# Splitting a dependency name in the layer norm and moving the first half's output store in a transformer layer on eight cores

## What is computed

```python
# x: (4, 4096, 1024)
x = x + 0.5 * ffn(layernorm(x), W1, b1, W2, b2)
x = x + attn(layernorm(x), Wq, Wk, Wv, Wo)
x = x + 0.5 * ffn(layernorm(x), W1, b1, W2, b2)

# ffn: weights are rounded to -1, 0, 1 first (clip(round(W / (mean|W| + 1e-5))))
h = relu(x @ quant(W1).T + b1)          # 1024 -> 4096
out = h @ quant(W2).T + b2              # 4096 -> 1024
# attn: 16 heads of 64; a query sees the keys of its own block of 64
#       and the 16 global keys at the start, causally
```

## Time and profile before

| what | value |
|---|---|
| times of the two runs shown | 2217.58 and 2296.53 us, median 2257.06 us |
| device time of the profiled execution | 2216.75 us |
| its span, core 0 (slowest) | 2215.2 us |
| spans of the eight cores | 2201.8 to 2215.2 us |
| TensorE busy | 1531.6 us, 69% of the span |
| mean granted TensorE clock, core 0 | 0.828 of full speed |

### The profile page before, as it was taken

The page is one execution under the profiler, slowest core; times in us unless marked ns, Lnnn a source line. Parts: engine busy times, 40 slices in busy tenths (PEclk is TensorE's granted clock), DMA queues, the critical chain, the costliest instruction groups (busy, mean ns, idle before and its releaser), DMA issues.

```text
span 2215.2 us, 22369 instructions; the slowest of 8 cores (2201.8 to 2215.2 us)
## 1 busy us (share of the span) xinstructions
PE 1531.6 (69%) x8576; PEld 726.5 (33%) x8676; DVE 547.6 (25%) x746; ACT 423.2 (19%) x601; POOL 84.8 (4%) x68
## 2 busy tenths in 40 slices
PE   1003124861984797898956987989569879895698
PEld 0001001430444343343533433435334334354343
DVE  4663553001034300202043002020430020204300
ACT  1001001212203220311222303112223031122230
POOL 0000000000003000000030000000300000003000
PEclk7556556985895898898968998999689989996799
DMA  6877886783112145342220444422204544222044
GB/s 195 289 266 252 257 251 199 237 266 143 53 62 77 38 148 167 103 152 76 76 77 19 152 152 134 152 76 77 77 17 147 154 139 147 82 76 77 6 148 151
DMA packets 218496, 297.31 MB, mean 134 GB/s; under 512 B 6164, under 2 KB 194582, under 8 KB 215064
## 3 DMA queue, kind: packets, MB, share of 16 engines
q1 hardware_dynamic: 188056, 253.93, 36.5%
q10 hardware_dynamic: 30336, 41.95, 5.7%
HBM read 262.31 MB, written 33.55 MB: 134 GB/s over the span
## 4 chain that ended last, share of the span: by engine, by line
PE 58%; DMA 20%; DVE 10%; ACT 5%; issue 4%; POOL 2%; SPq 0%; ACTq 0%; DVEq 0%; POOLq 0%
PE PSB L391 17%; PE PSB L346 17%; PE PSB L463 10%; PE PSB L482 5%; DMA w2q_s<-xsq 3%; PE PSB L749 3%; DMA vaug<-w2t 3%; DMA w1b<-w1q_s 2%; POOL psb L599 2%; DMA w1q_s<-xsq 1%; PE SA L222 1%; DMA xres<-xfm 1%; DMA h<-w1t 1%; DMA vaug<-wvt 1%; DMA vaug<-wkt 1%
## 5 line engine op out<-in xcount | busy, mean ns | idle before, releaser
L346 PE MATMUL PSB<-xhat,w1b 128*128 128x512 bf16 x2003 | 477.5, 397 | 147.8 <-DMA w1b<-w1q_s 115.8
L391 PE MATMUL PSB<-h,w2b 128*128 128x512 bf16 x2001 | 453.2, 381 | 19.0 <-DMA w2b<-w2q_s 14.3
L346 PEld LDWEIGHTS PSB<-xhat,w1b 128*128 128x128 bf16 x2048 | 203.4, 101 | 402.6 <-issue 187.0
L391 PEld LDWEIGHTS PSB<-h,w2b 128*128 128x128 bf16 x2048 | 196.0, 98 | 259.7 <-issue 35.3
L351 ACT ACTIVATE h<-PSB,b1s 128x512 bf16<-128x512 f32 x256 | 176.0, 687 | 530.7 <-PE PSB L346 291.3
L402 DVE SCALAR_TENSOR_TENSOR xres<-PSB,xres 128x512 f32<-128x512 f32 x64 | 44.3, 692 | 877.7 <-PE PSB L396 770.9
L463 PE MATMUL PSB<-xhat,pjb 128*64 128x512 bf16 x1024 | 230.3, 389 | 11.9 <-DVE xhat L268 11.9
L463 PEld LDWEIGHTS PSB<-xhat,pjb 128*64 128x64 bf16 x1024 | 114.8, 112 | 126.6 <-issue 23.5
L222 PE MATMUL SA<-xsq,onesmean 128*1 128x512 bf16 x96 | 36.1, 544 | 138.3 <-ACT xsq L214 138.3
L489 DVE CAST vaug<-PSB 64x512 bf16<-64x512 f32 x64 | 43.7, 683 | 293.2 <-PE PSB L482 290.2
L482 PE MATMUL PSB<-pjb,xhat 128*64 128x512 bf16 x512 | 112.8, 382 | 4.1 <-DVE vaug L489 4.1
(11 more groups left out here) (122 smaller groups left out, 966.8 us busy)
## 6 DMA issues: line engine op xcount, KB each, us to landing
w1b<-w1q_s SPq DMA_DIRECT2D x64, 1024.0 KB, 6.5
w2b<-w2q_s SPq DMA_DIRECT2D x64, 1024.0 KB, 6.3
h<-w1t SPq DMA_DIRECT2D x16, 2048.0 KB, 9.0
vaug<-w2t SPq DMA_DIRECT2D x32, 1024.0 KB, 6.5
pjb<-wk_s SPq DMA_DIRECT2D x10, 1024.0 KB, 6.0
xres<-xfm SPq DMA_DIRECT2D x8, 1024.0 KB, 7.3
pjb<-wq_s SPq DMA_DIRECT2D x8, 1024.0 KB, 10.5
pjb<-wv_s SPq DMA_DIRECT2D x8, 1024.0 KB, 6.0
```

The lines of the kernel that those rows point to most:

```text
L346: lambda e, lhs=lhs, c=c, pview=pview: e.matmul(pview, lhs, xhat[:, c * T:(c + 1) * T], start=(c == 0), stop=(c == NCH - 1)),
L391: lambda e, buf=buf, c2=c2, pview=pview: e.matmul(pview, buf[:, c2 * 128:(c2 + 1) * 128], h[:, c2 * T:(c2 + 1) * T], start=(c2 == 0), stop ...
```

## The change

It has two parts.

First, the two ScalarE copies of `ln` also write names of their own, `xb_lo` and `xb_hi`. The matmuls of L222 read `xb_lo` for the first four chunks and `xb_hi` for the last four, in place of `xb`. The squaring L217 reads both, so it waits for the same as before. No instruction moves in any engine's list; a wait does.

Second, the output store is recorded inside `ffn2`, in the call whose result is final (`store_t=t`, the second `ffn2` of each tile): the first half behind the addition for `k` = 3, the second behind that for `k` = 7. The transfer `w2dma(5)` is recorded at the end of iteration 3, so it stands behind the first half's store.

```diff
         def ln(xr, xrname, glob):
             em.op("scalar", ... activation(xsq[:, 0:2048], xr[:, 0:2048], AF.Copy),
-                  reads=["xr_lo"], writes=["xb"])
+                  reads=["xr_lo"], writes=["xb", "xb_lo"])
             em.op("scalar", ... activation(xsq[:, 2048:4096], xr[:, 2048:4096], AF.Copy),
-                  reads=["xr_hi"], writes=["xb"])
+                  reads=["xr_hi"], writes=["xb", "xb_hi"])
             em.op("vector", ... xsq * xsq
-                  reads=["xb"], writes=["sq"])
+                  reads=["xb_lo", "xb_hi"], writes=["sq"])
             for c in range(NCH):
                 em.op("tensor", ... L222
-                      reads=["xb", "onesmean"], writes=bk(0))
+                      reads=["xb_lo" if c < 4 else "xb_hi", "onesmean"], writes=bk(0))
...
-        def ffn2(xr, xrname, glob):
+        def ffn2(xr, xrname, glob, store_t=None):
...
+                if store_t is not None and (k == 3 or k == 7):
+                    hf = 0 if k == 3 else 1
+                    dst = bass.AP(yout.tensor, (hf * 4) * 128 * TOK + store_t * T,
+                                  [[TOK, 128], [128 * TOK, 4], [1, T]])
+                    dma(lambda e, dst=dst, xr=xr, hf=hf: e.dma_start(dst, ...),
+                        reads=[f"xr_{half}"], writes=[f"yout{store_t}{hf}"],
+                        sem=f"ys{hf}")
...
-                    ffn(xr, xrname, False)
-            for hf in range(2):
-                dma(... store of half hf ..., sem=f"ys{hf}")
+                    ffn(xr, xrname, False, store_t=t)
```

More of the change, by code:

```diff
@@ L405, in ffn2 @@
                       reads=bank + [f"xr_{half}"], writes=[f"xr_{half}"])
+                if store_t is not None and (k == 3 or k == 7):
+                    hf = 0 if k == 3 else 1
+                    dst = bass.AP(yout.tensor, (hf * 4) * 128 * TOK + store_t * T,
+                                  [[TOK, 128], [128 * TOK, 4], [1, T]])
+                    dma(lambda e, dst=dst, xr=xr, hf=hf: e.dma_start(
+                        dst, xr[:, hf * 4 * T:(hf * 4 + 4) * T].rearrange(
+                            "p (c k) -> p c k", c=4)),
+                        reads=[f"xr_{half}"], writes=[f"yout{store_t}{hf}"],
+                        sem=f"ys{hf}")
                 if glob:
@@ L427, in ffn2, with ffn @@
                     w2dma(k + 2)
-        def ffn(xr, xrname, glob):
+        def ffn(xr, xrname, glob, store_t=None):
             ffn1(xr, xrname, glob)
-            ffn2(xr, xrname, glob)
+            ffn2(xr, xrname, glob, store_t=store_t)
         def proj(glob):
@@ L986, in build_nc @@
                     ln(xr, xrname, False)
-                    ffn(xr, xrname, False)
-            for hf in range(2):
[L989 to L995, removed]
+                    ffn(xr, xrname, False, store_t=t)
+                else:
+                    for hf in range(2):
+                        dst = bass.AP(yout.tensor, (hf * 4) * 128 * TOK + t * T,
+                                      [[TOK, 128], [128 * TOK, 4], [1, T]])
+                        dma(lambda e, dst=dst, xr=xr, hf=hf: e.dma_start(
+                            dst, xr[:, hf * 4 * T:(hf * 4 + 4) * T].rearrange(
+                                "p (c k) -> p c k", c=4)),
+                            reads=[f"xr_{'lo' if hf == 0 else 'hi'}"],
+                            writes=[f"yout{t}{hf}"], sem=f"ys{hf}")
         em.final_wait(["ys0", "ys1"])
```

## The result

The profiled execution of the changed kernel took 2238.58 us, its longest span 2237.0 us; before it was 2216.75. Over repeated runs of both kernels the ratio after to before is 1.0101, with a 95% interval from 1.0081 to 1.0122. The change makes the kernel slower by 1.0%. That lies within the 2% of the forecast, but the forecast was no change, and this is clearly not nothing. Predicted were 2236 us, a ratio of 1.0087 to the profiled execution. Some executions are several per cent slower whatever the kernel, by its time also the one of 2296.53 us shown before, and the ratios leave them out.

What follows compares the result with a forecast made beforehand. TensorE held 58% of the chain of waits, DMA 20%, VectorE 10%. To 2216.75 us it added 8.0 for the norms, 8.8 for waits at chunk 5 and 2.1 for clock falls: 2236 us, range 2207 to 2270.

Steps and rivals of the forecast that it cites:

- no change: Whole kernel: 2236 us, 0.9% above the profiled execution, was taken as within the 2% a measurement can tell; chance 0.92.
- the sum: Whole kernel: 2216.75 + 8.0 for the norms + 8.8 for the waits + 2.1 for the clock = 2235.7 us.
- L228's clock level: Layer norm: half clock in L228 makes its 8 matmuls 3.57 us instead of 1.89, a norm 6.1 instead of 4.43.
- the norm term: Twelve layer norms, L217's to L237's start: ten at half clock in L228 give 70.0 us, +8.0; bounds -8.8 and +11.4.
- The 62.0: Twelve norms before the change, in us: 44.0 without idle time plus 11.1 idle ahead of L232 and 6.9 ahead of L237.
- the load norms: First norms of tiles 1 to 3, behind a tile load: four matmuls run early at L211's end, too thin to help.
- The store's position: Second `ffn2`, chunk 5: weights behind 1 MB of store on the same queue land 8.0 us after issue; alone, 5.2.
- the piling-up rival: Chunks 5 and 6 of the second `ffn2`: store and three weight transfers pile up, both wait, +48 us, 2265 us; chance 0.06.
- The move brought nothing elsewhere: Tile end, next tile's loads and chunk 7's weights: moving the store gains nothing; a shorter tile boundary would refute it.
- The size of the wait: Chunk 5 of the second `ffn2`: a stall of 2.2 us in each of four tiles, 8.8 us, bounds 0 and 13.6.
- the clock's chance: Behind the wait at chunk 5: one time in three the clock falls, about 1.6 us each, 2.1 us in four tiles.
- The rule on gaps: Layer norms: long idle gaps between matmul bursts lower the clock; read alone, it favours the change, norms summing to 53.2 us.

Runs made afterwards that it cites:

- the fillers: Unread matmuls, 16 in each of seven norms behind a layer, added to the kernel with only the names split: ratio 0.9973; added to the changed kernel: 1.0030.
- fill_all: Kernel before with the names split, store unmoved, plus unread matmuls in every gap of the norms behind a layer and behind tile loads: ratio 0.9922, rerun 0.9901.

## Why the prediction was right or wrong, point by point

**The step that failed: from the sum to "no change".** The sum gave 2236 us, 0.9% slower, and the measured 1.0% agrees with it. The forecast then went by "About 2% is what a measurement of this kernel can tell from no change, so I forecast no change". No number of the prediction supports that 2%; it had two runs 79 us apart and no measured spread. The repeated runs put the ratio at 1.0101 with an interval of 0.2% to each side, so the 0.9% of the sum could be told from nothing, and the change was slower. Inside the sum two terms were mis-sized as well, in opposite directions.

**What decides in the norm: right.** It named L228's clock level, and the three norms behind the attention as the place: foretold 6.1 us, measured 5.91 on average, 4.43 before. The idle time before L232 went to 0.0. The names alone, and the fillers, show it as cause.

**The size of the norm term: too large, and then not counted to its end.** The term is "10 of 12 norms at half clock in L228", +8.0 us. Measured are +4.3 from L217 to L237, 63.6 to 67.8, where the prediction had 62.0 to 70.0. The 62.0 put together from idle times of core 0 was low: that core's own sum is 62.9, the average of eight 63.6. Three more things differ. L228 was seldom slow to its last matmul (3.41 us, not 3.57). Tile 0's first two norms, where both halves come back to back, gained 0.3 and 1.05 us. And the load norms, which I had among the ten, had been slow before too: 5.86, 5.58, 5.57 before, 5.69, 5.36, 5.45 after. What I left out lies behind L237: from L217 to the next layer's first matmul the loss over eleven norms is +6.1. Of that 1.5 us lie behind L237; in the norm behind tile 1's attention L252's matmul took 0.58 us after the change and 0.37 before.

**The store's position: right.** "Behind 1 MB of store on the same queue" is what costs; the other queue and one place further back remove nearly all of it. Chunk 6 did not wait (step of 7.33 us), so the piling-up rival was wrong. The move brought nothing elsewhere: the next tile's first half landed after 8.2, 7.3 and 7.3 us in tiles 1 to 3 (average of eight cores), and after 8.1, 7.4 and 7.4 before. From the last addition of a tile to the next L211 it was 9.6, 8.7 and 8.7 us, and 9.5, 8.8 and 8.8 before.

**The size of the wait: near, the clock's chance: mis-sized.** The term 8.8 us for four waits of 2.2 stands against 8.1 us of waits with the store alone and 10.0 with both parts. The term that was wrong is the clock behind the wait: "I give it one time in three, 4 x 1.6 / 3 = 2.1 us." The price was near, 1.5 to 1.75 us in 17 of the 22 falls, up to 3.0 in the rest. The chance came from nothing in the trace of the kernel before: with both parts the clock fell in 22 of 32 waits, 5.3 us in four tiles, with the store alone in 4 of 32, 0.9 us. The store's part comes to 14.9 us, not 10.9.

**The rule on gaps.** The Trainium skill, TensorE: Matmul & The Clock Gate, "Why this matters for your kernels", spoke for the change. The gap did shrink, 3.01 to 2.06 us, and the clock fell all the same, behind the attention of tiles 1 to 3 on all eight cores, so here the rule read as a matter of the longest gap misleads. The same section's advice to keep the engine busy is borne out by the fillers.

**The sum.** 19.0 us foretold, 21.8 between the profiled executions. Norms 8.0 against 6.1, store 10.9 against 14.9: two errors of opposite sign, so that the total came within 3 us is in part luck. The loss of the two parts together, 21.0 us, also holds 5.9 us that neither showed alone, and the prediction had no term for that.

## What to carry to other kernels

An instruction that is let go earlier is worth its time only on the path; when it is the work that kept an engine's clock up, starting it early can make the next instruction slower, as L228 here. Before moving a wait, look at the granted clock of what comes after, not only at who waits for whom. And in this kernel a store on the queue that brings the next weights belongs behind them or on the other queue, however early its data is ready.

## What the runs showed that I had not expected

Unread matmuls paid for themselves: 444 more matmul records on the page of `fill_all` than on that of the changed kernel (9120 against 8676) and 2% less time than that kernel. The two clock losses also met, in one profiled execution of each kernel. The wait at chunk 5 cost 9.8 us by itself, 15.7 with the split names and 11.2 with these and the fillers, though nothing between the norm and chunk 5 had been changed.
